# A Perceiver-like block on one core: latent rows in two parts, four-operation key rotation, two rope-query banks, values product in three runs

## The reference

```
x += L0_xattn(norm(x), ctx)      # 16 heads, int8 fake-quantised projections
x += L0_attn(norm(x))            # differential attention, 16 heads of 2*64
x += L0_ffn(norm(x))             # gated, e4m3 rounding
x += L1_xattn(norm(x), ctx)      # masked cross attention, 16 heads of 16, output layer-normed
x += L1_attn(norm(x))            # latent attention (below)
x += L1_ffn(norm(x))             # squared relu, e4m3 rounding
```

```
q_c  = rmsnorm(x @ wq_down)   # 192      kv_c = rmsnorm(x @ wkv_down)   # 64
q_nope = q_c @ wq_up          # 16 x 128 q_rope = rope(q_c @ wq_rope)   # 16 x 64
k_nope, v = split(kv_c @ wkv_up)         # 16 x 128 each
k_rope = rope(x @ wk_rope)               # 64, shared by the heads
scores = (q_nope . k_nope + q_rope . k_rope) / sqrt(192);  softmax;  out = (probs @ v) @ wo
```

## Time and profile before

| what | value |
|---|---|
| median of 3 runs | 758.72 us |
| the profiled execution's own time | 758.8 us |
| its span, first to last instruction | 757.0 us |
| mean granted TensorE clock | 0.961 |
| TensorE busy | 677.9 us, 90% |
| VectorE, ScalarE, GpSimd busy | 422.8, 277.0, 75.9 us |
| X1 from its first full units to its last scores | 444 to 608.6 us |
| latent attention's loop | 643 to 719.5 us |

### The profile page before, as it was taken

One profiled execution on the slowest core, in us unless ns is written; L12 is line 12 of the kernel. 1 busy time (PEld: TensorE's weight loads), 2 busy tenths in 40 slices (PEclk: granted clock), 3 DMA queues, 4 the chain that ended last, 5 costly groups with the idle time before them and its releaser, 6 DMA issues.

```text
span 757.0 us, 21668 instructions
## 1 busy us (share of the span) xinstructions
PE 677.9 (90%) x9594; PEld 445.9 (59%) x9594; DVE 422.8 (56%) x981; ACT 277.0 (37%) x501; POOL 75.9 (10%) x137
## 2 busy tenths in 40 slices
PE   5999999999997999999969599899999977899744
PEld 3656656566565677667755357567576764366511
DVE  5234455666564655555534825346776845366477
ACT  1344434434442233334326334333444444121123
POOL 1020000001001111111112321010101002000000
PEclk9999999999999999999998889899999999999967
DMA  5242001106004400000006118411101000000000
GB/s 184 84 146 59 30 29 37 51 30 196 2 3 145 163 29 30 30 29 2 1 12 229 40 42 215 150 58 29 57 31 31 3 3 0 3 3 3 3 1 28
DMA packets 39357, 42.02 MB, mean 56 GB/s; under 512 B 13216, under 2 KB 29856, under 8 KB 39008
## 3 DMA queue, kind: packets, MB, share of 16 engines
q1 hardware_dynamic: 39264, 40.63, 17.1%
HBM read 40.10 MB, written 0.52 MB: 54 GB/s over the span
## 4 chain that ended last, share of the span: by engine, by line
PE 79%; DVE 13%; issue 3%; ACT 2%; POOL 1%; DMA 1%; SPq 0%; DVEq 0%; ACTq 0%; POOLq 0%
PE psum L347 15%; PE psum L353 14%; PE psum L1015 6%; PE psum L414 5%; PE psum L381 4%; PE psum L367 4%; PE psum L392 4%; PE psum L1062 4%; PE psum L1021 3%; PE psum L1660 2%; PE psum L1046 2%; PE psum L1679 2%; PE psum L1035 1%; PE psum L1636 1%; PE psum L1641 1%
## 5 line engine op out<-in xcount | busy, mean ns | idle before, releaser
L347 PE MATMUL psum<-arena 128*128 128x512 f32 x256 | 126.2, 621 | 9.1 <-DMA ident<-in_ident 8.6
L353 PE MATMUL psum<-arena 128*128 128x256 f32 x512 | 124.6, 390 | 0.4 <-ACT arena L577 0.4
L353 PEld LDWEIGHTS psum<-arena 128*128 128x128 f32 x512 | 94.9, 192 | 23.6 <-issue 9.2
L347 PEld LDWEIGHTS psum<-arena 128*128 128x128 f32 x256 | 46.4, 197 | 55.4 <-issue 43.5
L603 ACT ACTIVATE arena<-arena 128x512 f32<-128x512 f32 x64 | 48.6, 806 | 78.2 <-DVE arena L722 74.7
L722 DVE TENSOR_SCALAR arena<-psum 128x512 f32<-128x512 f32 x64 | 41.2, 685 | 33.6 <-PE psum L381 30.3
L414 PEld LDWEIGHTS psum<-arena 128*17 128x17 f32 x4096 | 39.4, 96 | 34.1 <-issue 28.2
L597 ACT ACTIVATE arena<-psum,arena 128x512 f32<-128x512 f32 x64 | 42.5, 688 | 37.9 <-DVE arena L709 37.8
L709 DVE TENSOR_REDUCE arena<-psum 128x1 f32<-128x512 f32 x64 | 42.4, 685 | 22.7 <-PE psum L367 22.6
L414 PE MATMUL psum<-arena 128*17 128x32 f32 x4096 | 45.7, 196 | 9.5 <-issue 4.9
L1015 PE MATMUL psum<-y_cols,arena 128*128 128x512 f32 x112 | 52.2, 599 | 0.0
(11 more groups left out here) (229 smaller groups left out, 984.2 us busy)
## 6 DMA issues: line engine op xcount, KB each, us to landing
arena<-in_ctxT SPq DMA_DIRECT2D x32, 512.0 KB, 3.6
arena<-in_L_attn_Wv SPq DMA_DIRECT2D x1, 2048.0 KB, 8.4
arena<-in_L_attn_Wq SPq DMA_DIRECT2D x8, 256.0 KB, 2.9
arena<-in_L_attn_Wk SPq DMA_DIRECT2D x8, 256.0 KB, 3.2
arena<-in_L_attn_Wo SPq DMA_DIRECT2D x1, 2048.0 KB, 11.8
arena<-in_L_ffn_w_gating SPq DMA_DIRECT2D x1, 2048.0 KB, 7.5
arena<-in_L_attn_wo SPq DMA_DIRECT2D x1, 2048.0 KB, 11.3
arena<-in_wq_upT SPq DMA_DIRECT2D x1, 1536.0 KB, 7.9
```

Of the source, the lines that this page charges most:

```text
L347: last = nc.tensor.matmul(bank, wkv[:, c, i * P:(i + 1) * P], x[:, c, :], start=(c == 0), stop=(c == NC - 1))
L353: last = nc.tensor.matmul(bank[:, kk * D:(kk + 1) * D], x[:, c, k * P:(k + 1) * P], wkv[:, c, D:2 * D], start=(c == 0), stop=(c == NC - 1))
```

## The change

1. X1's values product of a batch is issued in three runs: groups 0 and 1, then (behind the second half of the scores) group 2, then (behind a unit) group 3. ScalarE takes the product out behind exponentials 2 and 3, and the third unit stands before the turns.
2. The guests of the last tile's steps are put in another order. There are now guests on VectorE and GpSimd too: latent rows of tiles 0 to 2 (`HEAD`) are made while X1 ends, tile 3 (`LAST`) follows alone, and the turns and copies of the latents are in these two parts as well. Two folds stand before X1's last values product, five before the down projection of tile 3, one after it.
3. The weights of the rope keys are laid out on the host four times over (turned and signed), so the down projection has 448 columns, and the rotation is two products and two sums for the direct and the swapped form.
4. The rope query uses two banks in turn.
5. GpSimd clears the probability buffers behind the last latent rows.

The diff, cut to its core:

```diff
@@ xattn, pool
         if not L0:
             delta_power(g, NT - 1)
+            if after:
+                e.phases[M1].during_x1_pool(g)
@@ batch_cols_pe
         unit_pe(pe, slot(b, 0))
         if b:
-            all_values(pe, b - 1)
+            pe.wait_ge(s_exp, 4 * b)
+            values(pe, b - 1, 0), values(pe, b - 1, 1)
         scores_cols(pe, b, 1)
+        if b:
+            values(pe, b - 1, 2)
         unit_pe(pe, slot(b, 1))
+        if b:
+            values(pe, b - 1, 3)
         out_rows(pe, tile_at(b, TAKE))
+        unit_pe(pe, slot(b, 2))
         turn_taken(pe, tile_at(b, TURN))
         next_turn(pe, normed(b))
-        unit_pe(pe, slot(b, 2)), unit_pe(pe, slot(b, 3))
+        unit_pe(pe, slot(b, 3))
@@ xattn, pe, behind the loop
+            for i in range(2):
+                pe.wait_ge(s_ev[i], 2 * NB)
+            guest(pe, 0)
             all_values(pe, NB - 1)
             pe.wait_ge(s_mx, 4 * NB)
+            next_turn(pe, NT - 2)
             turn_taken(pe, NT - 1)
-            next_turn(pe, NT - 2)
-            guest(pe, 0)
+            guest(pe, 1)
             turn_out(pe, NT - 1)
-            guest(pe, 1)
+            guest(pe, 2)
             out_rows(pe, NT - 1)
-            guest(pe, 2)
+            guest(pe, 3)
             next_turn(pe, NT - 1)
@@ batch_cols_act
-        if b:
-            take_out(act, b - 1)
         exp_cols(act, b, 2), exp_cols(act, b, 3)
         for u in own(b, 0, 1):
             unit_act(act, u)
+        if b:
+            take_out(act, b - 1)
+        for u in own(b, 0, 2):
+            unit_act(act, u)
         next_cols(act, normed(b))
...
@@ xattn, dve, behind the loop
             rows_ready(v, last)
+            guest(v, 0)
             residual(v, last)
             delta_stats(v, last)
+            guest(v, 1)
             delta_add(v, last)
         v.sem_inc(done, 1)
         next_stats(v, last)
+        if not L0:
+            guest(v, 2)
         next_rows(v, last)
@@ mla
+DW = QR + KR + 3 * ROPE
...
+    HEAD, LAST = (0, 1, 2), (NT - 1,)
+    LAT = ([B[i][:, head] for i in (7, 6, 2, 3, 4)],
+           [B[i][:, a * P:(a + 1) * P] for i, a in ((5, 0), (0, 0), (5, 1), (5, 2), (0, 1))])
...
+    def mean_power(g, ts):
+        g.wait_ge(s_ms, 1 if ts is HEAD else 2)
+        nc.gpsimd.tensor_tensor(flat(rr), flat(ms), e.neghalf2[:, 0:2 * len(ts)], ALU.pow).then_inc(s_rms, 1)
+    def during_x1_pool(g):
+        mean_power(g, HEAD)
     def pool(g):
+        mean_power(g, LAST)
+        g.wait_ge(s_lat, 2)
         for u in range(2):
             nc.gpsimd.memset(pT[u].rearrange("p c t k -> p (c t k)"), 0.0).then_inc(s_zero, 1)
-        g.wait_ge(s_ms, 1)
-        nc.gpsimd.tensor_tensor(flat(rr), flat(ms), e.neghalf2, ALU.pow).then_inc(s_rms, 1)
@@ during_x1_pe
         if k == 0:
+            fold(pe, 0), fold(pe, 1)
+        elif k == 1:
             down(pe, 0), down(pe, 1)
-        elif k == 1:
-            down(pe, 2), fold(pe, 0)
+        elif k == 2:
+            down(pe, 2)
         else:
-            fold(pe, 1), fold(pe, 2), fold(pe, 3)
+            for j in range(2, PAIRS - 1):
+                fold(pe, j)
@@ queries
-            wait(pe, s_rope, 2 * j)
-            nc.tensor.matmul(QRB, wr[:, 0, cols], qcT[:, 0, :], start=True, stop=False)
+            wait(pe, s_rope, 2 * (j - 1))
+            nc.tensor.matmul(QRB[j % 2], wr[:, 0, cols], qcT[:, 0, :], start=True, stop=False)
@@ mla, pe
         down(pe, 3)
-        for j in range(4, PAIRS):
-            fold(pe, j)
-        pe.wait_ge(s_lat, 1)
-        pe.wait_ge(s_sq, 2 * NT)
-        for t in range(NT):
...
+        turn_latents(pe, HEAD)      # six matmuls a tile, as the loop before, into LAT[k]
+        fold(pe, PAIRS - 1)
         pe.wait_ge(s_wf, 3 * PAIRS)
+        turn_latents(pe, LAST)
...
@@ during_x1_act
         if k == 0:
-            squares(act, 0), squares(act, 1)
+            copy_fold(act, 0)
         elif k == 1:
-            squares(act, 2), copy_fold(act, 0)
+            copy_fold(act, 1), squares(act, 0)
+        elif k == 2:
+            squares(act, 1), squares(act, 2)
         else:
-            copy_fold(act, 1), copy_fold(act, 2), copy_fold(act, 3)
+            for j in range(2, PAIRS - 1):
+                copy_fold(act, j)
@@ mla, act
         squares(act, 3)
-        for j in range(4, PAIRS):
-            copy_fold(act, j)
...
+        copy_latents(act, 0)        # waits s_cols 1, three copies of the part's columns
+        copy_fold(act, PAIRS - 1)
+        copy_latents(act, 1)
@@ rope_rows
+        v.wait_ge(s_sq, 2 * (ts[-1] + 1))
+        for dst, table, a in ((t1, cosr, QR + KR), (t2, sinr, QR + KR + ROPE)):
+            e.ch.mark(nc.vector.tensor_tensor(dst[:, at, :], e.psum[:, 2 + ts[0]:3 + ts[-1], a:a + 2 * ROPE],
+                                              table.unsqueeze(1).to_broadcast([P, n, 2 * ROPE]), ALU.mult))
+        e.ch.join()
+        twice = lambda x: x.unsqueeze(2).to_broadcast([P, n, 2, ROPE])
+        for i in range(2):
+            a = slice(i * ROPE, (i + 1) * ROPE)
+            e.ch.mark(nc.vector.tensor_tensor(krow[:, 1 + i, at, :].rearrange("p t (u f) -> p t u f", u=2),
+                                              twice(t1[:, at, a]), twice(t2[:, at, a]), ALU.add))
@@ mla, dve
+    def during_x1_dve(v, k):
+        if k == 0:
+            v.wait_ge(s_w, 16 * N_W)
+            nc.vector.tensor_copy(identm, mask32).then_inc(s_mask, 1)
+            rope_rows(v, (0,))
+        elif k == 1:
+            mean_squares(v, HEAD)   # two operations, then s_ms
+        else:
+            latent_rows(v, HEAD)    # the three products by the power, waits s_rms
...
+    def dve(v, done):
+        rope_rows(v, (1, 2))
         e.ch.join()
         v.sem_inc(s_lat, 1)
+        mean_squares(v, LAST)
+        rope_rows(v, LAST)
+        latent_rows(v, LAST)
+        e.ch.join()
+        v.sem_inc(s_lat, 1)
+        turned_latents(v, 0)        # waits s_cols, two copies of the part's columns
+        turned_latents(v, 1)
```

More of the change, by code:

```diff
@@ L663, in batch_cols_act @@
             unit_act(act, u)
+        if b:
+            take_out(act, b - 1)
+        for u in own(b, 0, 2):
+            unit_act(act, u)
         next_cols(act, normed(b))
-        for u in own(b, 0, 2, 3):
+        for u in own(b, 0, 3):
             unit_act(act, u)
@@ L883, in dve @@
         else:
+            guest = e.phases[M1].during_x1_dve if after else lambda v, k: None
             rows_ready(v, last)
+            guest(v, 0)
             residual(v, last)
             delta_stats(v, last)
+            guest(v, 1)
             delta_add(v, last)
@@ L1624, in during_x1_pe, with turn_latents @@
         if k == 0:
+            fold(pe, 0), fold(pe, 1)
+        elif k == 1:
             down(pe, 0), down(pe, 1)
-        elif k == 1:
-            down(pe, 2), fold(pe, 0)
-        else:
-            fold(pe, 1), fold(pe, 2), fold(pe, 3)
+        elif k == 2:
+            down(pe, 2)
+        else:
+            for j in range(2, PAIRS - 1):
+                fold(pe, j)
+    def turn_latents(pe, ts):
+        k = 0 if ts is HEAD else 1
+        pe.wait_ge(s_lat, k + 1)
+        for t in ts:
+            r = slice((t - ts[0]) * P, (t - ts[0] + 1) * P)
+            nc.tensor.transpose(LAT[k][0][:, r], qc[:, t, 0:P], e.ident)
+            for i in range(2):
+                nc.tensor.matmul(LAT[k][1][half(i), r], qc[:, t, P:QR], e.ident, start=True, stop=True)
+            for i in range(3):
+                ins = nc.tensor.transpose(LAT[k][2 + i][:, r], krow[:, i, t, :], e.ident)
+        ins.then_inc(s_cols, 1)
     def queries(pe, j, i):
@@ L1684, in pe @@
         down(pe, 3)
-        for j in range(4, PAIRS):
-            fold(pe, j)
-        pe.wait_ge(s_lat, 1)
-        pe.wait_ge(s_sq, 2 * NT)
-        for t in range(NT):
-            r = slice(t * P, (t + 1) * P)
-            nc.tensor.transpose(LAT[0][:, r], qc[:, t, 0:P], e.ident)
-            for i in range(2):
-                nc.tensor.matmul(LAT[1][half(i), r], qc[:, t, P:QR], e.ident, start=True, stop=True)
-            for i in range(3):
-                last = nc.tensor.transpose(LAT[2 + i][:, r], krow[:, i, t, :], e.ident)
-        last.then_inc(s_cols, 1)
-        pe.wait_ge(s_wf, 3 * PAIRS)
-        pe.wait_ge(s_qc_act, 1)
-        pe.wait_ge(s_qc_dve, 1)
+        turn_latents(pe, HEAD)
+        fold(pe, PAIRS - 1)
+        pe.wait_ge(s_wf, 3 * PAIRS)
+        turn_latents(pe, LAST)
+        pe.wait_ge(s_qc_act, 2)
+        pe.wait_ge(s_qc_dve, 2)
+        pe.wait_ge(s_kv_dve, 2)
+        pe.wait_ge(s_kv_act, 4)
         for j in range(2):
@@ L1775, in rotate @@
         for i, dst in enumerate((qcos, qsin)):
-            nc.vector.tensor_tensor(blocks(dst[j % 3]), blocks(QRB), rope[:, i, :].unsqueeze(1).to_broadcast([P, NB, SQ]),
+            nc.vector.tensor_tensor(blocks(dst[j % 3]), blocks(QRB[j % 2]), rope[:, i, :].unsqueeze(1).to_broadcast([P, NB, SQ]),
```

(11 more changed lines are left out.)

81 lines of the change are left out of this document (33 added, 48 removed).

## The result

The changed kernel takes 749.22 us (median of 4 runs, 748.55 to 749.82), beside 759.02 us for the kernel before in runs on the same chip (758.57 to 759.66). The ratio is 0.9861, with a 95% interval of 0.9844 to 0.9879: faster by 1.4%. The forecast was 748.0 us, in a range of 743.5 to 756.5.

What follows compares the result with a forecast made beforehand. TensorE was taken to bound the second cross attention and latent loop, a chain across engines the handover. Terms -2.4 - 5.8 - 2.8 = -11.0 us from 758.8 gave 747.8, said as 748; likeliest 744 to 752, with rival 1 743.5 to 756.5.

Steps and rivals of the forecast that it cites:

- Values product: Second cross attention: three runs cost 5.4 us and take away 7.8 us of stalls and half clock, sum -2.4.
- Rival 4: Batches 2 to 6: context loads hold up instruction supply, the split moves stalls and adds one, 761 us; chance 0.08.
- Handover: Between second cross attention and latent loop: reordered work brings the first rope query from 642.97 to 637.2, -5.8 us.
- The folds in the hole: Handover: two folds, 2.9 us, hidden in the 3.3 us hole before the last values product, keeping TensorE at work.
- the wait for the seventh fold's copies: Handover: ScalarE's three copies of the last of five folds hold up the columns' copy by 1.0 us, to 628.15.
- the waits of 1.2 and 1.0 at the end: Handover: short TensorE holes around the last fold, forecast at 1.2 and 0.9 us.
- rival 2: Handover: the clock drops behind short TensorE holes, costing 1.7 to 3.4 us, about 751 us; chance 0.08.
- Clears: Handover: GpSimd's clears moved behind the last latent rows, normalised rows take 0.41 instead of 1.90 us, -1.5.
- The choice of 0 for the clears at their new place: Handover: clears beside VectorE's PSUM copies and first rotation priced at 0, with 1.5 us as upper bound.
- Rotation: Handover: four-operation key rotation, price 0 for tiles 1 and 2, gain in the last tile; 448 columns cost 0.43 a tile.
- Two banks: Latent attention's loop: four rope-query waits for VectorE's rotation go, -2.8 us, between -1.4 and -2.8.
- The sum: Whole kernel: -2.4 - 5.8 - 2.8 = -11.0 us against 758.8, giving 747.8, stated as 748.

Runs made afterwards that it cites:

- e14: The kernel before with only the six head-weight loads of the latent attention issued one at each of contexts 7 to 12: 753.2 us, ratio 0.9915.
- e11: The changed kernel with the six head-weight loads issued one at each of contexts 7 to 12 instead of all behind context 6: 746.19 us, ratio 0.9832.
- e12: e7 with the six head-weight loads issued one at each of contexts 7 to 12: 743.24 us, ratio 0.9779.
- e5: The changed kernel with values groups 2 and 3 both behind the second half of the scores, so two runs of 64: 749.23 us, ratio 0.9846.
- e7: e5 with the seventh fold behind the last row turn and the last latents' turn waiting only for seven folds' copies: 744.97 us, ratio 0.9797.
- e1: The changed kernel with the values product back in one run per batch, take-out and third unit back too: 750.22 us, ratio 0.9866.
- e10: The kernel before with only the values product in three runs and its order changes on ScalarE and TensorE: 757.34 us, ratio 0.9968.
- e13: The changed kernel with the head-weight loads spread over contexts 7 to 12 and the values product in one run per batch: 746.63 us, ratio 0.9835.
- e3: The changed kernel with GpSimd's two clears back at the start of its list for the latent attention: 747.69 us, ratio 0.9868.
- e4: The changed kernel with the old ten-operation key rotation and 320 columns in the down projection: 746.4 us, ratio 0.9829.
- e2: The changed kernel with the rope query in one bank again: 749.98 us, ratio 0.9876.
- e8: The kernel before with 43 more turns (86 TensorE instructions) at the start of the second cross attention: 760.25 us, one execution.

## Why the prediction was right, point by point

- **Values product, forecast -2.4, measured -3.2 for the batches.** The cost: 0.66 + 0.36 + 0.36 is 0.13 over 1.25, and the change of tile 0.19, so 0.32 x 15 = 4.8; without stalls and lost clock the stretch is 4.3 longer (152.5 against 148.2, the latter from e14). Forecast 5.4, slightly dear. The gain: the stalls went from 4.9 to 1.3 us and the half-clock stretch went. The forecast had all of the 4.9 go, and for one cause, the length of the run. That cause fits the two short stalls only, and for them the loads of the context are not ruled out. The long one hangs on the loads that fill the DMA engines (e11, e12 and e14 have none near 480). In the three runs it shrank from 2.6 to 1.3 or less and left the clock alone, while two runs of 64 did not shrink it (3.0 in e5, 2.6 in e7); that three runs spend the instructions already at hand more slowly is a reading and was not tested. So the term came near its number partly by luck: the same split was worth 0.6 us in e1 and 3.6 in e10, and a shift of 86 instructions moved the batches by 5.3. Rival 4 had named loads (of the context) as the cause of a late instruction supply, with the wrong outcome. The page "Runtime: NRT & Kernel Launch" of the Trainium skill (Instruction fetch mechanics) calls the crossing of a block mostly hidden. The trace agrees with "mostly": 3 of the 22 fetches in the batches of the kernel before go with a stall. It does not bear out what the forecast drew from the page, that a run of 256 instructions could not run dry: the three stalls are 1.1 to 2.6 us, and 3.3 in e1.
- **Handover, forecast -5.8, measured -5.7.** The first rope query was forecast at 28.6 us behind the last scores. It came 28.6 us behind the end of the last batch and 29.3 behind the last scores, because two groups of values of the batch before now stand behind them; the forecast did not count these 0.7 us. The folds in the hole, the wait for the seventh fold's copies, and the waits of 1.2 and 1.0 at the end stand in the trace as forecast. Clock drops (rival 2) did not come in this profile. Of the eight profiles with this order of the handover (after, e1 to e5, e11, e13) they came in three, e1, e3 and e5: 3.4 us at half clock behind the last holes of 1.2 and 1.0 us, so 1.7 us. The forecast's chance of 0.08 for rival 2 was low.
- **Clears, a step of -1.5.** The duration was right (1.45 beside them, 0.41 without), its worth was not: the folds and copies set the time, and moving the clears gained nothing there (e3). My sum took this in, since it let the folds end later than the rows; as a step by itself it should have been priced at 0. The choice of 0 for the clears at their new place was right: the copies beside them kept their time.
- **Rotation, priced at 0.** Its 1.7 us of TensorE time were in the sum as wider down projections, but not set against what they bought, which was nothing (e4).
- **Two banks, forecast -2.8, measured -2.6 for the loop.** All four waits went; e2 brought back 2.8 of waits and 2.4 of time.
- **The sum** missed by 1.2 us of median. The stages agree to -11.5 against -11.0. The difference is the untouched part ahead, 2.2 us longer in the profiled execution, with a stretch of half clock more (3.4 us near 243, which costs 1.7). In the other profiles, e8 with its added turns apart, the batches began at 448.7 to 451.6, the later ones (450.7 to 451.6) with this stretch and the others without it, so it is scatter.

## What to carry to other kernels

When the busiest engine shows "issue" stalls inside runs of short instructions, look at the DMA share ahead of each before reordering the instructions: spreading a 5 MB load over six batches took the long stall away in a few lines. Before crediting a reordering with the stalls that it removes, shift the instruction stream without reordering it and see how much that alone moves. Keep tiled groups together, since each island costs 0.2 us. Price a faster operation only against the wait that ends last there: the four-operation rotation and the moved clears were faster by their own rows and gained nothing or lost.

## What the runs showed of the hardware

- TensorE's instructions come in packets of 16 KB, one for about 250 instructions, which take 0.9 to 1.5 us in the batches of the kernel before. After a stall TensorE goes on 1.3 to 1.5 us after the packet has landed (before, e1, e5, e7). Ten runs of 128 matmuls with 128 weight loads had a packet start within 0.6 us of their start, and nine stalled, by 0.7 to 2.0 us; of about seventy runs of 64 or 32 so placed, away from the full DMA engines near 480, none stalled by more than 0.4.
- At the end of a time with full DMA engines (a share of 1.07 to 1.10 over 20 us in before, e1 and e5) the packet starts late: TensorE had been dry for 0.2 to 0.9 us when it did, and the stall was 2.6 to 3.3 us. In the short stalls of the kernel before, and in the stall of 1.3 us of the changed kernel, it starts about 1.2 us before TensorE runs dry.
- Half clock of 3.4 to 6.8 us followed the stalls of 1.8 us or more in the batches (e13 1.8, e8 2.0, e7 and before 2.6, e5 3.0, e1 3.3). The stall of 1.3 us in the changed kernel was not followed by it. Length of the idle time alone does not decide: the holes of 1.2 and 1.0 us at the end of the handover were followed by half clock in e1, e3 and e5 and not in the changed kernel.
- GpSimd's clears slowed a VectorE operation with SBUF alone on both sides from 0.41 to 1.45 us (e3), and operations that read PSUM not at all (0.61, 0.62 and 0.55 us with and without them).
